# Attention over a 4096-node graph: all queries made in the prologue, values made among the first head's score slots, two value visits per step

## What is computed

```python
h = jnp.maximum(_layernorm(x, axis=-1), 0.0)           # x: 4096 x 256, float32
adj = jnp.maximum(adjacency_matrix, eye)               # adj: 4096 x 4096
q = jnp.einsum('nd,hdk->hnk', h, Wqs)                  # 8 heads, key width 64
k = jnp.einsum('nd,hdk->hnk', h, Wks)
v = jnp.einsum('nd,hdk->hnk', h, Wvs)
scores = jnp.einsum('hqk,hmk->hqm', q, k) * kd ** (-0.5)
scores = scores + IDENTITY_BIAS * eye - MASK_VAL * (1.0 - adj)
att = jax.nn.softmax(scores, axis=-1)
return x + jnp.einsum('hqm,hmk,hko->qo', att, v, Wo)
```

## Time and profile before

| | |
|---|---|
| median of 3 executions | 2731.86 us (2731.72 to 2733.88) |
| the profiled execution's own time | 2723.36 us |
| span of its program | 2721.9 us |
| PE busy | 2651.4 us (97%) |
| DVE busy | 2261.7 us (83%) |
| ACT busy | 1850.8 us (68%) |
| POOL busy | 1278.2 us (47%) |

### The profile page before, as it was taken

How to read it: one execution, slowest core, us unless ns; L and a number is a source line. 1 busy time by engine, 2 the same in 40 slices (tenths; PEclk the granted TensorE clock), 3 DMA queues, 4 the chain that set the end, 5 groups by cost and what they waited for, 6 DMA issues and landing times. The chain is left out here.

```text
span 2721.9 us, 58724 instructions
## 1 busy us (share of the span) xinstructions
PE 2651.4 (97%) x17344; PEld 1881.8 (69%) x17344; DVE 2261.7 (83%) x3833; ACT 1850.8 (68%) x3041; POOL 1278.2 (47%) x2418
## 2 busy tenths in 40 slices
PE   7899999999999999999999999999999999999997
PEld 5566677777777767676666777777777777777775
DVE  6788888888888888888848888888888888888885
ACT  3566767767677676676746776767676767777774
POOL 2356555565665556666412434343434444444433
PEclk9999999999999999999999999999999999999999
DMA  6367776676876667777552656565566666565654
GB/s 166 106 143 182 176 171 170 167 174 152 186 183 165 169 166 175 158 174 183 147 149 77 151 142 164 144 157 143 131 146 151 153 153 155 137 145 136 153 143 105
DMA packets 263358, 418.51 MB, mean 154 GB/s; under 512 B 98944, under 2 KB 119936, under 8 KB 259200
## 3 DMA queue, kind: packets, MB, share of 16 engines
q1 hardware_dynamic: 172032, 228.88, 32.7%
q0 software_dynamic: 89088, 184.69, 30.1%
q10 hardware_dynamic: 2176, 4.19, 0.4%
HBM read 136.31 MB, written 46.27 MB: 67 GB/s over the span
## 5 line engine op out<-in xcount | busy, mean ns | idle before, releaser
L310 POOL DMA_DIRECT2D S<-S x2048 | 1005.6, 499 | 1182.9 <-DVE S L735 1132.3
L714 DVE CUSTOM_DVE_ANT_0 S<-psS,B 128x1024 f32<-128x1024 f32 x1024 | 1223.1, 1217 | 201.1 <-PE psS L452 140.9
L600 ACT ACTIVATE S<-S,negm 128x1024 f32<-128x1024 f32 (+1 forms) x768 | 1097.4, 1429 | 101.4 <-DVE negm L721 100.0
L607 ACT ACTIVATE PT<-psT 128x512 f32<-128x512 f32 x1024 | 606.6, 593 | 253.6 <-PE psT L465 242.0
L452 PE MATMUL psS<-K,QH 128*128 128x512 f32 x2048 | 718.6, 432 | 29.8 <-DVE mx L714 26.9
L735 DVE STREAM_TRANSPOSE S<-S 128x2048 f32<-128x2048 f32 x256 | 590.3, 2306 | 104.6 <-PE psO L489 103.3
L452 PE MATMUL psS<-K,QL 128*128 128x512 f32 x2048 | 642.2, 395 | 0.0
L465 PEld LDWEIGHTS psT<-ident,S 128*128 128x128 f32 x4096 | 472.2, 141 | 223.0 <-issue 123.1
L465 PE MATMUL psT<-ident,S 128*128 128x128 f32 x4096 | 615.7, 278 | 7.4 <-ACT S L600 4.9
L475 PE MATMUL psO<-PT,V 128*64 128x256 f32 x4096 | 520.4, 385 | 0.0
L489 PE MATMUL psO<-S,V 128*64 128x256 f32 x4096 | 470.3, 382 | 1.5 <-DMA S<-S 1.5
(11 more groups left out here) (51 smaller groups left out, 971.7 us busy)
## 6 DMA issues: line engine op xcount, KB each, us to landing
S<-S SPq DMA_DIRECT2D x2048, 64.0 KB, 3.0
S<-S POOLq DMA_DIRECT2D x2048, 64.0 KB, 2.9
B<-in_adj POOLq DMA_DIRECT2D x128, 256.0 KB, 6.5
bias_scratch<-B SPq DMA_DIRECT2D x32, 1024.0 KB, 6.0
B<-bias_scratch SPq DMA_DIRECT2D x128, 256.0 KB, 4.9
hq<-hT_scratch SPq DMA_DIRECT2D x32, 256.0 KB, 3.6
RB<-rden_scratch SPq DMA_DIRECT2D x128, 64.0 KB, 3.3
S<-in_x SPq DMA_DIRECT2D x8, 512.0 KB, 3.7
```

Source lines behind the costliest of these rows:

```text
L310: pool.dma_start(dst, src).then_inc(late_sent[q][half], 16)
L600: nc.scalar.activation(part, part, ACT.Exp, bias=negm[:, h % 2, q:q + 1], accum_out=sums[:, h % 2, q, e:e + 1]).then_inc(probs_ready, 1)
L607: nc.scalar.activation(PT[:, s % RING, :], psT[s % 2][:, :], ACT.Copy).then_inc(pt_act, 1)
L714: nc.vector.tensor_tensor_reduce(out=part, in0=psS[j % 2][:, :], in1=B[:, q, k * SLOT:(k + 1) * SLOT], scale=SCALE, scalar=LOWEST, op0=ALU ...
```

## The change

- **Queries.** The prologue makes keys and queries of every chunk. The queries take the place of the values in `keys_values`: two matmul pairs of 512 columns. `psS` is now shared: of each of the two tiles one bank holds keys (`psK[pair]`) and the other queries (`psQ[pair]`), where the keys had both before. ACT rounds 128 x 512 queries into a stage `QS` (twice per chunk), DVE subtracts (twice per chunk), and SP stores high and low part of each pair to a DRAM scratch `QX` (`store_q`, two DMAs of 512 KB per chunk). In the steps SP loads the queries of the head that comes three later (`load_q`, two DMAs of 128 KB per step) into `Q`, which has room for two heads. `query`, its copies and `hq` are gone.
- **Values.** They are made behind the prologue from `hT`, which SP loads again (`load_hv`, 512 KB for each of eight chunks, four buffers): chunks 0 to 3 behind each pair of the first head's score slots, chunks 4 to 7 behind the second head's first two slots.
- **Steps.** The three value visits become two: slots 0 to 3 in one visit behind the score slot that follows `T3`, slots 4 to 7 at the end as before. The projection stands between the last two score slots of a step, where it stood behind both. On ACT the exponentials of half 1 both follow the copy of slot 7.

```diff
     def sync_program(sp):
+        def store_q(i, b):
+            for pair in range(GROUP // 2):
+                sp.wait_ge(q_lo, i * GROUP + ((b + 1) * (GROUP // 2) + pair + 1))
+                sp.dma_start(QX[g, pair, :, :, bass.ds((i * 2 + b) * CH, CH)], QS.bitcast(F32)[:, b, pair, :, :]).then_inc(q_stored[b], 16)
+        def load_q(i, h):
+            e = h % 2
+            rows = QX[g, h // 2, e * KD:(e + 1) * KD, :, bass.ds(i * QW, QW)]
+            for half in range(2):
+                sp.dma_start(Q.bitcast(F32)[half * KD:(half + 1) * KD, e, :, :], rows).then_inc(q_in[e], 16)
...
                 if norm:
                     sp.wait_ge(x_transposed, i * 2 + b + 1)
-                else:
-                    sp.wait_ge(v_proj, i * 4 + (2 * b + 2 + START))
-                load(i + 1, b)
+                    load(i + 1, b)
+                store_q(i, b)
+                if not norm:
+                    load(i + 1, b)
...
+        load_weights(Wv, wv, wv_in)
+        for n in range(4):
+            load_hv(n)
+        for b in range(2):
+            store_q(NC // 2 - 1, b)
+        sp.wait_ge(q_stored[0], 16 * (GROUP // 2 + START))
+        load_q(0, 0)
+        load_q(0, 1)
...
-            if h == 1 and more:
-                sp.wait_ge(q_proj, count(i, 4, 1, 0))
-                load_hq(i + 1)
+            if more or h + 3 < GROUP:
+                sp.wait_ge(scores_ready, count(*ahead(i, h, 1), SLOTS, SLOTS))
+                load_q(*ahead(i, h, 3))
...
     def tensor_program(pe):
...
+            for pair in range(GROUP // 2):
+                pe.wait_ge(q_lo, i * GROUP + (b * (GROUP // 2) + pair + 1))
+                for c in range(DC):
+                    last = nc.tensor.matmul(psQ[pair], wq[:, c, pair * P:(pair + 1) * P], hc[b][:, c, :],
+                                            start=(c == 0), stop=(c == DC - 1))
+                last.then_inc(q_proj, 1)
...
+        for n in range(SLOTS // 2):
+            scores(0, 0, 2 * n, True)
+            scores(0, 0, 2 * n + 1, True)
+            value_rows(n)
+        scores(0, 1, 0)
+        scores(0, 1, 1)
+        for n in range(SLOTS // 2, NC):
+            value_rows(n)
```

More of the change, by code:

```diff
@@ L95, in group_programs @@
     x_v = x.rearrange("(n r p) d -> n p r d", p=P, r=CR)
-    psK = [[psS[pair][:, b * BANK:(b + 1) * BANK] for b in range(2)] for pair in range(GROUP // 2)]
+    psK, psQ = ([psS[pair][:, b * BANK:(b + 1) * BANK] for pair in range(GROUP // 2)] for b in range(2))
     psV = [psO, psP]
@@ L424, in keys_values @@
                     for c in range(DC):
-                        last = nc.tensor.matmul(psV[u][:, a * 256:(a + 1) * 256], hc[b][:, c, m * P:(m + 1) * P],
+                        last = nc.tensor.matmul(psV[u][:, a * 256:(a + 1) * 256], hv[n % 4][:, c, m * P:(m + 1) * P],
                                                 wv[:, c, :], start=(c == 0), stop=(c == DC - 1))
                 last.then_inc(v_proj, 1)
-        def query(i, h, wait_hq, free, first=False):
-            if wait_hq:
-                pe.wait_ge(hq_in, i * 16 + 16)
-            pe.wait_ge(q_lo, count(i, h, 1, 0))
-            if not free:
-                pe.wait_ge(head_added, count(i, h, 1, START - 4))
-            for c in range(DC):
-                last = nc.tensor.matmul(query_psum(first)[:, 0:QW], wq[:, c, h * KD:(h + 2) * KD], hq[:, c, :],
-                                        start=(c == 0), stop=(c == DC - 1))
-            last.then_inc(q_proj, 2)
         def scores(i, h, j, first=False):
@@ L638, in scalar_program @@
         act.sem_inc(v_act, START)
+        for b in range(2):
+            act.sem_inc(q_stored[b], 16 * START)
         if norm:
@@ L647, in scalar_program @@
         act.sem_inc(pt_act, PT_START)
-        for k in range(NE):
-            exps(0, 0, 0, k)
-        for k in range(NE - 1):
-            exps(0, 0, 1, k)
+        value_rows(0)
+        value_rows(1)
+        exps(0, 0, 0, 0)
+        exps(0, 0, 0, 1)
+        value_rows(2)
+        exps(0, 0, 0, 2)
+        value_rows(3)
+        exps(0, 0, 1, 0)
+        exps(0, 0, 1, 1)
+        for n in range(4, NC):
+            value_rows(n)
         steps(act, step)
@@ L812, in vector_program @@
                 dve.wait_ge(h_out[b], 16 * (NC // 2 + START))
-        for j in range(SLOTS):
-            mask(0, 0, j, first=True)
-        for q in range(QT):
-            transpose_late(0, 0, q, False)
+        for n in range(SLOTS // 2):
+            mask(0, 0, 2 * n, first=True)
+            mask(0, 0, 2 * n + 1, first=True)
+            if n == 2:
+                for b in range(2):
+                    dve.wait_ge(q_stored[b], 16 * (GROUP // 2 * (NC // 2) + START))
+                transpose_late(0, 0, 0, False)
+            value_rows(n)
         mask(0, 1, 0)
         mask(0, 1, 1)
+        transpose_late(0, 0, 1, False)
+        for n in range(SLOTS // 2, NC):
+            value_rows(n)
         steps(dve, step)
```

233 lines of the change are left out of this document (107 added, 126 removed).

## The result

The changed kernel takes 2795.09 us in the median (2791.05 to 2815.42, 4 executions) against 2731.79 us of the kernel before beside it: a ratio of 1.0249 (of the means; that of the medians is 1.023), 95% interval 1.0198 to 1.030. It is slower by 63 us, where 2737 was forecast with 2711 to 2757 as the range. The profiled execution's own time is 2796.63 us, its span 2795.1.

A forecast was written before the change was run, and what follows sets the result against it. PE was taken to bound the steps, late moves next. Steps -57 against prologues +63 (chunks +12 and +1, gaps +11, clock +4, values +17 and +18) gave 2729, said as 2737 for the median; range 2711 to 2757.

The forecast's parts named there:

- The steps: what goes.: Steps: queries and one value visit leave PE, 1.46 us less per pair of steps, 45.3 us in each group.
- The steps: what comes.: Steps: new query loads and later slots delay the late moves; net gain 20 us in second group, 35 in first.
- they start about 2.5 before it; I take 0.9 us of wait: Second group's h = 3: moves start about 2.5 us before T0, PE waits 0.9 us, 15 times, 13 us.
- Two more DMAs fit: Steps without bias loads in SP's queue: some 3 us are free before the next moves, so both query loads fit.
- I add 10: First group's steps: 10 us of waits added to its 28.5, leaving 35 us gained, bounds 50 and 20.
- First prologue, chunks.: First prologue: the load of x waits behind query stores, chunk period 10.1 us for 7.7, five times: +12, bounds +8 and +20.
- The gap ahead of the first scores.: Before the first scores, twice: PE waits about 7.0 us for query stores and loads, +5.6 each, bounds +4.5 and +7.5.
- the 2 us for the clock: At the gap ahead of the first scores: PE cools and runs at half clock, 2 us each, bounds 0 and 3.4.
- Values among the slots.: First score slot to first late values: 51.7 us for 34.55, +17.1 in the first group, +18 in the second.
- B: Rival: SP's queue holds the steps and the x loads, 60 x 0.2 + 7 = +19, 2756 us; chance 0.25.
- C: Rival: PE's idle time in first-prologue chunks and both gaps brings half clock, +13, 2750 us; chance 0.10.
- A: Rival: the late moves keep up, steps gain nearly their bounds, -83, 2711 us; chance 0.20.

The follow-up runs named there:

- the order by itself: Kernel before with only the step order changed (two value visits, projection between the last score slots), queries still made in the steps: 2704.1 us, ratio 0.9894.
- one statement moved up: Changed kernel with the steps' two query loads issued behind the store of rden, ahead of the wait for its landing: 2749.1 us, ratio 1.0050.
- all three kernels: Changed kernel with step query loads, chunk loads and first queries issued earlier; two, one or no adjacency loads between first group's move halves: 2715.3, 2711.6, 2726.2 us.

## Why the prediction was wrong

**The steps: what goes.** Right. Gap-free steps are 18.41 and 19.29 us (predicted 18.39 and 19.29), and the order by itself is worth 26 us.

**The steps: what comes.** Here the prediction failed: -57 predicted, +0.8 measured. That is 58 of the 67 us by which the profiled execution misses the forecast made for it, and the prologues are the other 10. The miss in the medians is 58 because the 8.5 us added for the median, which here stands 1.5 below the profiled execution, hide the prologues' part; that is luck. The failing sentence is "they start about 2.5 before it; I take 0.9 us of wait". In the second group's h = 3 the moves start 0.87 before `T0`, and the wait is 2.0 us a step, 30 us in all for 13. Against 3.69 before, the two issues take 1.3, the earlier `T0` 0.6, and the later load of `RB` (15.72 after the `T0` of h = 2, for 15.05) 0.7, together 2.6 of 2.8: I had counted the issues, and little of the other two, and started from one step with 4.04 where the mean is 3.69. The price had an error of its own: without query loads the moves start 2.50 before `T0`, which is the start that I forecast, and the step waits 0.25 us, not 0.9. So the price was too high for its start, and the start was wrong by more than that. The second group's h = 2, at 0.7 a step or 10.5 us, was sized right (12). Its sum of 20 became 4.7.

The first group is the larger part. "Two more DMAs fit", said of h = 0 and 1 by a step of the second group, doesn't hold for the first group's h = 1, which costs 0.90 a step; a move there takes 4.9 us to land even without query loads, 2.6 in the second group's h = 1, and SP's 2 MB of bias stores stand ahead of it (that they are the cause was not tested). And "I add 10" to the waits of before was a guess where a rule was at hand: h = 2 was already held by a transfer, the moves behind the adjacency loads, so whatever PE saves in it is lost, all 1.16 us of it (21.34 before, 21.47 after). Against their free times the first group's steps wait 0.90, 2.18 and 2.28 in h = 1, 2, 3, that is 15 x 5.36 = 80 us, where 28.5 + 10 were taken. Its -35 became +5.5.

**First prologue, chunks.** +17.5 for +12, within its bounds. The statistics of the last chunk start at 79.8 for 62.3. The term that was small is the landing of `x`, 6.0 us from the end of the low queries for 5.0, which makes the period 11.1 for 10.1 in each of five chunks; the store issued ahead of it landed at 44.93 and the load at 46.49. The upper bound, 6.6 behind all of the stores, was nearer. The Trainium skill's rule of ring order (DMA: Bandwidth & Descriptors, Queues, rings and completion order) was the better guide: the trace agrees in that the load lands behind both stores. I had priced it at 6 us more, for four periods where my own sum has five, which is 8; 5.5 more were measured.

**The gap ahead of the first scores.** 6.20 us for about 7.0, that is 5.0 more than the 1.22 of before for 5.6 (7.0 less 1.22 would be 5.8). But the way from the last chunk's statistics to the first scores grew by 7.8 (29.4 for 21.6). 4.1 of it lie between the last chunk's keys and the first scores: the gap, less a query's 0.9 that stood there before. 1.0 is a later normalisation. 2.7 is a stretch of half clock: from the last chunk's transposes to the next keys PE takes 7.07 us (88.87 to 95.94), in a middle chunk 4.36 (52.81 to 57.17). No term stood for this one; the 2 us for the clock are spent on the stretch behind the gap.

**Values among the slots.** 53.8 us for 51.7 + 2 in the first group, 53.6 in the second; 51.1 once the gap and its half clock are gone, so the clock costs 2.7 there. Right. The two prologues together came out +72.7 for +63.

**The rivals.** B, that SP's queue holds the steps and the `x` loads, is what happened; it was given 0.25 and a price of 2756, from 60 steps at 0.2 us. The held steps pay 0.7 to 2.3 us each; the 0.2 was an assumption with no row under it. C is seen in part: PE's granted clock falls to half in four stretches of the first prologue. PE had idled in them or just before: for 7.46 us until 39.27, 2.39 until 72.54, 3.44 until 88.87 and 6.20 until 109.17.

```profile
36.00:44.00 8.00, 4.73 (x13) 2.56 (x14) 6.88 (x19) 0.80 (x2) 1.01 (x1) 0.57 0.34 123
73.00:78.00 5.00, 4.85 (x15) 2.69 (x14) 3.47 (x8) 1.87 (x4) 0.00 (x0) 0.66 0.69 224
88.00:95.00 7.00, 6.13 (x14) 3.64 (x15) 3.59 (x6) 1.68 (x3) 4.88 (x6) 0.54 1.02 285
108.00:115.00 7.00, 5.83 (x14) 4.64 (x15) 2.47 (x4) 0.00 (x0) 0.00 (x0) 0.51 0.15 46
```

The first two cost nothing that shows beside the wait for `x`, which bounded the same chunks: both chunks took 10.9 us, the others 11.1 and 11.2. The third and the fourth stand behind the last such wait and cost 2.7 us each. A, that the moves keep up, is true only of the order alone.

**The markers.** 62 steps of the second group took 1207.9 us (1193 predicted, under 1175 for A), of the first 1246.8 (1207); the idle time for `x` was 3.3 us (2), the gap 6.2 (7). The mask waited for moves in h = 1 of the first group, which I had named as the mark of B.

**Open.** Why executions of one kernel differ by up to 24 us. Whether a queue's own order matters at all for the moves: no kernel issued full loads from another queue at exactly SP's time.

## What to carry to other kernels

When a bound engine is relieved, ask of every step whether the engine or a transfer ends it now; a step that a transfer holds keeps its length, and one just short of it goes over. Give each transfer that is nearly late a budget from its own rows (when its issue starts, how long it lands) and charge to it each DMA that is newly issued ahead of it on its engine, its bytes, and the time by which the consumer comes earlier. Take this budget as a mean over the steps and not from one of them. Loads that nobody waits for soon belong into a stretch where the issuing engine waits anyway: one statement moved up was worth 46 us here. Where waits grow, look at the granted clock of the steps too, since the waits can cost twice.

## What the runs showed of the hardware

- Two loads of 128 KB issued ahead delay small moves by SP's issue (1.3 us) and by their bytes (0.3 to 0.8 us of a landing of about 5). With 8 KB in place of 128 KB an issue takes as long: 1.29 us for two in both.
- Issuing the same loads from ACT's queue left the landing of SP's moves where it was (5.46 us for 5.24 in the first group's h = 1).
- Loads from POOL's queue delay SP's moves too. SP starts its moves of half 1 at the same time in all three kernels (1.4 us after `T0` in the first group's h = 2); one takes 6.5 us to land in the mean with two adjacency loads issued ahead by POOL, 5.0 with one, 3.2 with none.
- A 512 KB load that SP issued behind two 512 KB stores landed 4.5 to 4.9 us after its issue and 1.4 to 1.9 behind the second store; issued ahead of the stores, 3.4 to 3.7.
- PE's granted clock fell to 0.50 (1.2 GHz) during or just behind idle times of PE of 2.4 to 7.5 us, in the prologue and in steps. A score slot then took 2.07 us for 1.17.
